# Attention and mixture-of-experts layer on one core: where the first group's row maxima, its loads and the last routing stand

## What is computed

```python
x = L0_attn_x                                   # [4, 1024, 256]
xn = _layernorm(x, axis=-1)
x = x + _L0_attn_ref(xn, W_qkv, b_qkv, W_out, b_out) + _L0_ffn_ref(xn, w_gate, w1_e, w3_e, w2_e, w1_s, w3_s, w2_s)
# attention: 16 heads of 16, rotary embedding on q and k, softmax over 1024 keys, output projection
# ffn: sigmoid gate over 16 experts in 4 groups; the 2 best groups (by the sum of their two best), 4 experts a token,
#      swiglu experts (256 to 128 to 256) weighted and summed, and a shared swiglu of width 256
```

## Time and profile before

| | us |
|---|---|
| median of the three runs | 1383.35 |
| lowest, highest | 1358.87, 1412.32 |
| span of the profiled execution | 1217.1 |
| own time of the profiled execution | not recorded |

### The profile page before, as it was taken

How to read it: one execution, slowest core, us unless ns; L and a number is a source line. 1 busy time by engine, 2 the same in 40 slices (tenths; PEclk the granted TensorE clock), 3 DMA queues, 4 the chain that set the end, 5 groups by cost and what they waited for, 6 DMA issues and landing times. The chain is left out here.

```text
span 1217.1 us, 27786 instructions
## 1 busy us (share of the span) xinstructions
PE 1150.2 (95%) x8310; PEld 582.5 (48%) x8311; DVE 959.9 (79%) x1451; ACT 750.6 (62%) x1568; POOL 578.9 (48%) x861
## 2 busy tenths in 40 slices
PE   4999767999999999999999999998999999998998
PEld 2555422333333333333333333333788887875665
DVE  6575685999999999999999999970555555556888
ACT  3666303888888888888888888887333333330000
POOL 6999947354465653232322323231576666661000
PEclk9999955999999999999999999999999999999999
DMA  6466743454435453343324332402777666655765
GB/s 221 156 202 216 224 110 140 180 163 125 126 106 145 125 143 86 87 109 96 94 80 117 89 95 79 103 29 64 215 225 228 205 204 213 194 165 185 234 220 173
DMA packets 127288, 181.74 MB, mean 149 GB/s; under 512 B 41441, under 2 KB 88929, under 8 KB 125282
## 3 DMA queue, kind: packets, MB, share of 16 engines
q1 hardware_dynamic: 111842, 138.55, 39.6%
q0 software_dynamic: 15360, 42.04, 10.0%
HBM read 99.71 MB, written 80.81 MB: 148 GB/s over the span
## 5 line engine op out<-in xcount | busy, mean ns | idle before, releaser
L1048 DVE TENSOR_REDUCE mx<-pm 128x1 f32<-128x1024 f32 x512 | 620.6, 1222 | 31.4 <-PE pm L1098 30.6
L1022 ACT ACTIVATE pr<-pst 128x512 f32<-128x512 f32 x1024 | 556.6, 596 | 86.3 <-PE pst L1109 34.9
L1098 PE MATMUL pm<-kt,qt 48*128 48x512 f32 x1024 | 386.6, 461 | 13.4 <-DMA qt<-s_q 8.0
L1109 PE MATMUL pst<-qt,kt 50*128 50x512 f32 x1024 | 377.7, 449 | 6.5 <-DMA qt<-s_m 6.5
L1121 PE MATMUL po<-pr,vt 128*17 128x256 f32 x4096 | 322.9, 388 | 9.9 <-ACT osb L1032 9.6
L1098 PEld LDWEIGHTS pm<-kt,qt 48*128 48x128 f32 x1024 | 157.1, 192 | 237.5 <-DVE mx L1048 173.1
L1274 POOL DMA_INDIRECT s_y<-ys_c,slot_c x144 | 139.6, 969 | 85.7 <-issue 46.4
L1121 PEld LDWEIGHTS po<-pr,vt 128*17 128x17 f32 x4096 | 69.0, 95 | 198.9 <-issue 110.3
L1109 PEld LDWEIGHTS pst<-qt,kt 50*128 50x128 f32 x1024 | 152.8, 186 | 18.8 <-ACT pr L1022 10.9
L950 POOL DMA_INDIRECT s_xg<-p_rows,p_slot x128 | 125.2, 978 | 56.0 <-issue 29.8
L1354 PE MATMUL pd<-w13s,xt_c 128*128 x576 | 149.5, 382 | 0.4 <-ACT xt_c L1284 0.4
(11 more groups left out here) (188 smaller groups left out, 1169.5 us busy)
## 6 DMA issues: line engine op xcount, KB each, us to landing
xg<-s_xg SPq DMA_DIRECT2D x144, 128.5 KB
yg<-s_y SPq DMA_DIRECT2D x32, 512.0 KB, 3.9
s_q<-stg SPq DMA_DIRECT2D x32, 256.0 KB
s_k<-stg SPq DMA_DIRECT2D x32, 256.0 KB
kt<-s_k SPq DMA_DIRECT2D x32, 256.0 KB
qt<-s_q SPq DMA_DIRECT2D x64, 128.0 KB
s_o<-osb SPq DMA_DIRECT2D x32, 256.0 KB, 6.9
w13s<-w SPq DMA_DIRECT2D x1, 4608.0 KB, 14.6
```

The costliest lines, as they stand in the source:

```text
L1022: nc.scalar.activation(pr[:, (k % 2) * 4 + ORDER[i], :], pst[bank(gg, k, i)][:, :], ACT.Exp, scale=SCALE).then_inc(exp_ok, 1)
L1048: nc.vector.tensor_reduce(mx[:, half, col:col + 1], pm[slot][:, :, :].rearrange("p a n -> p (a n)"), AX.X, ALU.max).then_inc(mx_free, 1)
L1098: mm = pe.matmul(pm[slot][:, kk, :], qt[buf][rows, half, pair, qi * P:(qi + 1) * P], kt[buf][rows, pair, kk * 512:(kk + 1) * 512], start=T ...
L1109: pe.matmul(pst[bank(buf, k, i)][:, :], kt[buf][rows, pair, kc * P:(kc + 1) * P], qt[buf][rows, half, pair, :], start=True, stop=True)\
```

## The change

- Fourteen of group 0's maxima are done inside the projections, one a step in steps 24 to 37, on PE behind `back` and on DVE ahead of `rest`. They use one pair of banks, pm0, which now exists in both programs; for it pT and pV have one bank instead of two.
- The other eighteen are the prologue of attention, and the quads 0 to 3 of group 0 have none. The prologue's transposition of the first sixteen stands behind its fourth maximum.
- The first loads stand in steps 18, 19, 24 and 28, and in steps 32 and 33 the keys and the first half of the queries of group 1. In attention SP starts with `rows(0, 0, 0)`; the staging stores come behind it and the remaining loads of group 1.
- The routing of batch 3 stands in attention, on DVE behind the prologue's maxima; POOL's `choose` waits for it. The counting matmuls stand in quad 13 of group 0, into pm0, and that quad's four pm matmuls behind it. POOL's planning and sending stand two half groups later.
- Behind the last step PE has four matmuls into pQ whose result isn't used (FILL). DVE sets po to zero at the start of attention.
- The loops of the projections are written out; SP, DVE and POOL write out one group pair more in attention.

```diff
+FIRST_LOADS = 18
+FILL = 4
+IN_A = 14
+EARLY = {n: 1 for n in range(38 - IN_A, 38)}
...
-            def first_loads(k, t, b):
-                n = k - 3 * TPB
-                if n == 0:
+            def first_loads(n):
+                if n == FIRST_LOADS:
                     for i in range(2):
                         sp.wait_ge(st_out[i], STORES * 16)
-                    for i in range(TPB):
-                        sp.wait_ge(v_out[i], 16)
-                    load_keys(sp, s_k, first["kt"][0], 0, first["qk_in"])
-                if n == 2:
-                    load_queries(sp, s_q, first["qt"], 0, 0, first["qk_in"])
-                if n == 4:
-                    load_queries(sp, s_q, first["qt"], 1, 0, first["late_in"])
-                if n == 6:
-                    load_values(sp, s_v, first["vt"], 0, 0, first["v_in"])
+                    load_keys(sp, s_k, first["kt"][0], 0, first["qk_in"][0])
+                if n == FIRST_LOADS + 1:
+                    load_queries(sp, s_q, first["qt"][0], 0, 0, first["qk_in"][0])
+                if n == FIRST_LOADS + 6:
+                    load_queries(sp, s_q, first["qt"][0], 1, 0, first["late_in"][0])
+                if n == NT - 4:
+                    for i in range(TPB):
+                        sp.wait_ge(v_out[i], 16)
+                    load_values(sp, s_v, first["vt"][0], 0, 0, first["v_in"][0])
+                if n == NT:
+                    load_keys(sp, s_k, first["kt"][1], 1, first["qk_in"][1])
+                if n == NT + 1:
+                    load_queries(sp, s_q, first["qt"][1], 0, 1, first["qk_in"][1])
...
+            for n in range(NT + BACK):
+                if n >= BACK:
+                    back(n - BACK, (n - BACK) % TPB, (n - BACK) // TPB)
+                early(n, 0)
+                if 0 <= n - TURN < NT:
+                    turn(n - TURN, (n - TURN) % TPB, (n - TURN) // TPB)
+                k = n - PROJ
+                if 0 <= k < NT:
+                    project(k, k % TPB, k // TPB)
...
+            pe.wait_ge(qks_ok, NT)
+            for _ in range(FILL):
+                pe.matmul(pQ[0][:, :], xt[:, TPB - 1, 0, :], wsb[:, 0, 0:2 * C], start=True, stop=True)
...
-            load_keys(sp, s_k, kt[1], 1, qk_in[1])
-            load_queries(sp, s_q, qt[1], 0, 1, qk_in[1])
+            rows(0, 0, 0)
             load_queries(sp, s_q, qt[1], 1, 1, late_in[1])
             load_v(1, 0, 1)
-            store_half(sp, s_q, s_k, first["stg"], B - 1, 0, first["st_out"][0])
-            rows(0, 0, 0)
-            store_half(sp, s_q, s_k, first["stg"], B - 1, 1, first["st_out"][1])
+            for hh in range(2):
+                store_half(sp, s_q, s_k, first["stg"], B - 1, hh, first["st_out"][hh])
...
-            for use in range(AHEAD):
-                if use == FIRST_ROWS:
-                    turn_rows(0, 0, 0)
-                maximum(use, use % 2, use)
+            nc.vector.memset(po[:, :], 0.0).then_inc(po_ok, 1)
+            for use in range(IN_A, 32):
+                row_maximum(nc, dve, first, use, use % 2, use)
+                if use == 17:
+                    turn_rows(nc, dve, first, 0, 0, 0)
+            routed = Chain(dve, first["dve_own"])
+            routed.base = first["setup"] + ROOT_LINKS + (B - 1) * ROUTE_LINKS
+            for piece in range(5):
+                route(nc, dve, routed, first["gb"], keep, B - 1, piece, first["ex_ok"], first["ex_used"], keep["passed_dve"])
+            dve.sem_inc(route_ok, 1)
...
+                        counting = g == 0 and k == COUNT
+                        if counting:
+                            counts(place(g, k, 0) - 1)
```

More of the change, by code:

```diff
@@ L98, in rounds, with rounds_last @@
         emit(j)
-def rounds_last(eng, n, emit):
-    emit(0)
-    with eng.Fori(1, n - 1) as j:
+def rounds_last(eng, n, emit, head):
+    for j in range(head):
+        emit(j)
+    with eng.Fori(head, n - 1) as j:
         emit(j)
@@ L340, in _ @@
             setup = own.n
+            first["setup"] = setup
             def other_stats(k, t, b):
-                if not isinstance(k, int):
+                if b:
                     return
@@ L375, in routing, with early @@
                 assert t != TPB - 1 or own.n == ROUTE_LINKS, own.n
-            steps(dve, B, TPB, NT, [(0, other_stats), (BACK, rest), (TPB, routing)])
+            def early(n, spot):
+                use = early_use(n, spot)
+                if use is not None:
+                    row_maximum(nc, dve, first, use, 0, use)
+            for n in range(NT + BACK):
+                t, b = n % TPB, n // TPB
+                if n < NT:
+                    other_stats(n, t, b)
+                early(n, 0)
+                if n >= BACK:
+                    rest(n - BACK, (n - BACK) % TPB, (n - BACK) // TPB)
+                early(n, 1)
+                early(n, 2)
+                if TPB <= n < NT:
+                    routing(n - TPB, t, b - 1)
         @block.scalar
@@ L472, in back, with early @@
                 mm.then_inc(qrT_ok, 1)
-            steps(pe, B, TPB, NT, [(BACK, back), (TURN, turn), (PROJ, project)])
+            def early(n, spot):
+                use = early_use(n, spot)
+                if use is None:
+                    return
+                if use == 0:
+                    pe.wait_ge(first["qk_in"][0], LOAD)
+                for kk in range(2):
+                    max_half(pe, first, 0, use, 0, use, kk, use)
+            for n in range(NT + BACK):
+                if n >= BACK:
+                    back(n - BACK, (n - BACK) % TPB, (n - BACK) // TPB)
+                early(n, 0)
+                if 0 <= n - TURN < NT:
+                    turn(n - TURN, (n - TURN) % TPB, (n - TURN) // TPB)
+                k = n - PROJ
+                if 0 <= k < NT:
+                    project(k, k % TPB, k // TPB)
+                early(n, 1)
+                if 0 <= k < NT:
+                    project_v(k, k % TPB, k // TPB)
+                early(n, 2)
+            pe.wait_ge(qks_ok, NT)
+            for _ in range(FILL):
+                pe.matmul(pQ[0][:, :], xt[:, TPB - 1, 0, :], wsb[:, 0, 0:2 * C], start=True, stop=True)
 def store_half(eng, s_q, s_k, stg, b, hh, done):
@@ L1003, in body @@
                             send(*tile)
-            for j in range(3):
+            for j in range(4):
                 body(j)
-            with pool.Fori(3, NG // 2 - 1) as j:
+            with pool.Fori(4, NG // 2 - 1) as j:
                 body(j)
@@ L1162, in body @@
                                 pv(pb, pk, q - 1, 2 * g + pk // 8 if k else 2 * g - 1, m)
+                        if counting:
+                            pe.wait_ge(keep_ok, 2)
+                            for m in range(2):
+                                for kk in range(2):
+                                    max_half(pe, first, mbuf, us[m], m, place(g, k, m), kk, place(g, k, m) - 1)
+            pe.wait_ge(late_in[0], LATE)
+            for use in range(IN_A, 32):
+                for kk in range(2):
+                    max_half(pe, first, 0, use, use % 2, use, kk, IN_A if use < IN_A + 2 else use - 1)
             for j in range(NG // 2):
```

299 lines of the change are left out of this document (162 added, 137 removed).

## The result

The changed kernel took 1413.58 us (median of 4 runs, 1404.49 to 1424.06) beside 1388.62 us for the kernel before (4 runs, 1358.87 to 1412.32): ratio 1.0329, 95% interval 1.0199 to 1.0459. The forecast was 1375.9 us, 7.5 us under the 1383.35 us known then. The changed kernel is instead slower, by 25 us if one goes by the medians; the interval excludes no change, and just fails to show 2%.

What follows compares the result with a forecast made beforehand. PE, busy 1150.2 of 1217.1 us, was taken as the bound. A gain of 10.5 us at the loop's start less 3 us for counting made -7.5 us, 1383.35 to 1375.9 us; range 1348 to 1402.

Steps and rivals of the forecast that it cites:

- parts 1, 2 and 4: Early loads, early maxima in the projections' last tiles, and attention's shorter prologue: loop start at 187.9 instead of 198.4, 10.5 us gained.
- no gain, no loss: Loop's first quads: half clock until 14.9 us into the loop, costing 6.4 us, taken to happen again unchanged.
- part 5: Counting moved from the prologue to quad 13 of group 0: price 3 us, between 1.2 and 5.
- Parts 1 and 2: Projections: early loads delay SP's stores, 8 us taken; fourteen early maxima make a tile 4.48 us, hidden within those 8.
- The rival on half clock in the projections: Longer standstills at tiles 20, 24, 28 bring half clock, 7.5 us each: 1390.9 with two, 1398 with three; chance 15%.
- Part 3: End of projections: transposes, last early maximum and four filling matmuls (3.7 us); program end 165, 6 us later than before.
- clock stays high: Rival: full clock lasts after the fill into prologue and loop, gain 6.4 less 1.4 us, 1370.9; chance 15%.
- Part 4: Attention's prologue: 18 maxima instead of 24 at 1.27 us, loop start at 187.9 instead of 198.4.
- I leave what lies around the span as it is: Outside the profiled span: 166.25 us between span and the runs' median 1383.35, kept unchanged in the sum.
- the 256 quads are not shortened: Attention loop: a quad costs PE 2.44 us with or without its two maxima, so removing maxima from four gains nothing.
- Two rivals' prices: SP's queue hides the loads: 3.5 us better, 1372.4, chance 13%; full queue slows key issues: 3.6 worse, 1379.5, 17%.

## Why the prediction was wrong

The forecast was 7.5 us faster; on the quiet chip the profile is 23.9 us slower, 31.4 us off. Four steps of the prediction failed and make 26.4 of them: what is gained at the loop's start (parts 1, 2 and 4: 10.5 forecast, 1.35 measured), the clock in the loop's first quads ("no gain, no loss": 4.3 us lost), the price of the counting (part 5: 3 us forecast, 8.5 measured), and GpSimd's planning, which had no term (7.5 us). Step by step:

- **Parts 1 and 2, projections +6 us (159 to 165).** This failed first. Measured +14.9 at attention's first maximum. The size of the early maxima was right (a tile 4.65 us, forecast 4.48), as was the shape of SP's delay, whose price I put at 8 us where the early loads, without early maxima, make 18.5 (171.80 against 153.32 with late loads). What wasn't in the step at all: when the operands of the first maximum land. PE waited 6.27 us for them and did the tile behind at half clock, so that one step cost 14.6 instead of 4.1 us. The rival on half clock in the projections had the mechanism, and ascribed it to the stores.
- **Part 3, fill 3.7 us.** It took 5.85 us, half clock at its start and full at its end, and about 3.9 us of the time to attention's first maximum. The rival "clock stays high" was right for the prologue's first 5 us; then, with PE idle for 0.4 us at each maximum, the clock fell to half again.
- **Part 4, loop start.** The prologue was shortened by 16.2 us (36.8 to 20.6), forecast 15.4 (38.3 to 22.9): right. With the stage ahead of it 9 us worse than forecast, the gain of 10.5 shrinks to 1.35. A good part of it is not the maxima: before, PE waited 4.82 us for rows held by SP's queue.
- **"I take it that this happens again: no gain, no loss", the clock in the loop's first quads.** This failed. I took the half clock as a delay from the loop's start. It lasted 12.8 us before and 22.0 after (34 with 32 maxima in the prologue), and with matmuls put back into the four empty quads, 9. Price 4.3 us here. On the page TensorE: Matmul & The Clock Gate of the Trainium skill (What's actually happening) activity is what releases the throttle; I used that rule for the prologue alone and missed its bearing on quads that I had just emptied. These runs agree with it in direction: 9 us of half clock with the added matmuls, 21 without.
- **Part 5, counting 3 us, at most 5.** 8.5 us in the second and third half group. The wait on PE was of the size forecast, 1.31 us; the 17 us at half clock behind it were not in the sum, though the earlier trace rows show such a fall behind a standstill. With the wait filled, 1.6 us are left of the 8.5.
- **GpSimd's planning two half groups later.** It stood in the description of the change and had no term. 7.5 us in the fifth and sixth half group: a split queued behind a wait for VectorE's quad 4.
- **"I leave what lies around the span as it is", 166.25 us.** Also wrong, though it moved no term: 1.5 us lie around a span. A profile of 1217.1 beside runs of 1359 and more shows different conditions, and the sum was made from a profile that wasn't of those runs.
- The seventh to ninth half group add 2.6 us (2.1 of them the gap of 2.07 us at 397.90), the last two programs 1.7, the fourth half group 0.9; none was traced to its cause.

Together: -1.35 + 4.3 + 8.5 + 0.9 + 7.5 + 2.6 - 0.2 + 1.7 = 23.9 us. That the 256 quads are not shortened, PE being the limit beside VectorE, held.

The range has a slip of its own. By its rule (1366 to 1398, half of the runs' spread of 53.45 us on either side) it would be 1339 to 1425, not 1348 to 1402, and 1413.58 would lie inside, by the spread and not by any mechanism that the prediction priced. Two rivals' prices are off by a few tenths: 8 - 4.7 is 3.3, not 3.5, and 11.1 - 8 is 3.1, not 3.6.

Open: what disturbs the one kind of chip. In the profile after, PE stands still for 1.0 to 4.9 us, mostly 24 to 29 us apart, from 346 us on, with ScalarE or nothing visible named, and the loop's mean clock is 0.82. The kernel before is slowed as much there (1390.6 us), but no profile of it was taken on such a chip.

## What to carry to other kernels

Where PE is 95% busy, a change ahead of the loop is worth what the clock makes of it: price every new wait of over a microsecond with the half clock that may follow (here 0 to 7 us), and be wary of thinning out PE's work where its clock is still low. Where a queue has no slack, moving a load ahead of stores that someone waits for costs their delay, and the load's own landing decides when its first user can run: find both in the trace before counting the work that it feeds. When a profile's span and the runs' times differ by more than the few microseconds that lie around a span, the profile is of another condition.

## What the hardware showed that was not expected

- The same program took 1214 us on one chip and 1391 us on another, spans 1.5 us below either; granted clock 0.97 and 0.87 to 0.90.
- Gaps of 1.31, 1.59 and 1.80 us in a loop at full clock were followed by 17, 13 and 8 us at half clock (10 us in another profile of the same kernel behind the same 1.31 us); gaps of 1.93 and 2.07 us were followed by none, the granted clock staying at 1.00.
- PE stayed at half clock for up to 34 us of nearly unbroken work at the loop's start (33.74 us busy in 34.00 at 0.50).
- Full clock came about 4 us into the eight pQ matmul records of the fill, and was gone 7 us later, in a stretch in which PE was busy for 3.55 of 6 us.
- With keys and queries issued ahead of them (4.65 us of issues), the same eight store issues took 12.0 instead of 8.6 us.
